# Second attention, odd steps: output tile 0 is added between the rotation's second and third operation

## What is computed

```python
q = (q_latent @ Wqb)                       # per head 64 plain + 64 rotated
r_even = x_even * cos - x_odd * sin        # the rotation of q's second half
r_odd  = x_odd * cos + x_even * sin
scores = (q @ k.T) * scale                 # causal, softmax over keys
attn   = softmax(scores) @ v
x      = x + attn @ Wo                     # summed over the heads
```

## Time and profile before

| | us |
|---|---|
| median of 3 runs | 2337.33 (2334.87 to 2339.34) |
| the profiled execution, its own time | 2336.27 |
| its span in the trace | 2334.5 |
| TensorE busy | 2239.7 (96% of the span) |
| TensorE weight loads busy | 1939.0 (83%) |
| VectorE busy | 1823.8 (78%) |
| ScalarE busy | 1202.2 (51%) |
| GpSimd busy | 938.5 (40%) |

### The profile page before, as it was taken

The page is one execution under the profiler, slowest core; times in us unless marked ns, Lnnn a source line. Parts: engine busy times, 40 slices in busy tenths (PEclk is TensorE's granted clock), DMA queues, the critical chain, the costliest instruction groups (busy, mean ns, idle before and its releaser), DMA issues. The chain is left out here.

```text
span 2334.5 us, 41914 instructions
## 1 busy us (share of the span) xinstructions
PE 2239.7 (96%) x12798; PEld 1939.0 (83%) x12798; DVE 1823.8 (78%) x4052; ACT 1202.2 (51%) x2803; POOL 938.5 (40%) x757
## 2 busy tenths in 40 slices
PE   7999999999999999999999889999999999988997
PEld 6888888888888888887897668888888888867895
DVE  7777777777777777876676769998999898986776
ACT  4555555555554555552434356566566566642434
POOL 6444444456444434355222333243334243344223
PEclk9999999999999999999999999999999999999999
DMA  3455555545433332226984100000000000017876
GB/s 129 175 202 201 201 191 180 180 165 186 143 114 118 118 118 103 95 93 247 317 279 178 54 20 1 20 20 19 0 19 19 0 19 10 27 72 262 293 252 241
DMA packets 106767, 296.63 MB, mean 127 GB/s; under 512 B 9480, under 2 KB 11912, under 8 KB 101024
## 3 DMA queue, kind: packets, MB, share of 16 engines
q1 hardware_dynamic: 85792, 239.61, 29.6%
q0 software_dynamic: 11360, 37.76, 4.1%
q10 hardware_dynamic: 9504, 17.85, 2.3%
HBM read 150.20 MB, written 144.98 MB: 126 GB/s over the span
## 5 line engine op out<-in xcount | busy, mean ns | idle before, releaser
L74 PE MATMUL bank<-wo_hi,hq_hi 128*128 128x512 f32 x576 | 234.6, 407 | 15.2 <-DVE x L1514 14.6
L74 PE MATMUL bank<-xT_hi,w_hi 128*128 128x512 f32 x584 | 232.8, 399 | 8.1 <-DVE xT_lo L202 5.0
L76 PE MATMUL bank<-xT_hi,w_lo 128*128 128x512 f32 x584 | 229.7, 393 | 0.0
L75 PE MATMUL bank<-xT_lo,w_hi 128*128 128x512 f32 x584 | 229.4, 393 | 0.0
L76 PE MATMUL bank<-wo_hi,hq_lo 128*128 128x512 f32 x576 | 226.4, 393 | 0.0
L75 PE MATMUL bank<-wo_lo,hq_hi 128*128 128x512 f32 x576 | 225.6, 392 | 0.0
L1604 POOL TENSOR_TENSOR qf<-ra,rb 64x512 f32<-64x512 f32 x64 | 82.4, 1287 | 327.0 <-DVE rb L1707 326.7
L1427 ACT ACTIVATE s<-s,top 128x128 f32<-128x128 f32 (+3 forms) x256 | 141.0, 552 | 97.5 <-DVE top L1506 97.5
L862 DVE SCALAR_TENSOR_TENSOR x<-bank,inv,x 128x512 f32<-128x512 f32 x256 | 179.8, 742 | 13.3 <-PE bank L76 13.3
L1514 DVE SCALAR_TENSOR_TENSOR x<-bank,inv,x 128x512 f32<-128x512 f32 x256 | 179.8, 743 | 3.0
L873 DVE TENSOR_TENSOR hq_lo<-bank,hq_hi 128x512 fp32r<-128x512 f32 (+1 forms) x144 | 80.3, 567 | 116.1 <-ACT arena L729 60.9
(11 more groups left out here) (348 smaller groups left out, 7282.5 us busy)
## 6 DMA issues: line engine op xcount, KB each, us to landing
sorted_x<-blank SPq DMA_DIRECT2D x48, 1584.0 KB, 11.4
arena<-split_w SPq DMA_DIRECT2D x32, 1024.0 KB
split_w<-arena SPq DMA_DIRECT2D x48, 512.0 KB, 3.2
w_raw<-dram_wa SPq DMA_DIRECT2D x32, 512.0 KB, 4.9
raw<-dram_wr SPq DMA_DIRECT2D x24, 512.0 KB, 5.7
wo_raw<-dram_woa SPq DMA_DIRECT2D x32, 256.0 KB, 4.2
ctok<-dram_wva SPq DMA_DIRECT2D x16, 512.0 KB, 5.2
arrived<-routed_y SPq DMA_DIRECT2D x8, 1024.0 KB, 8.0
```

The lines of the kernel that those rows point to most:

```text
L74: nc.tensor.matmul(out, hi, mov_hi, start=first, stop=False)
L75: nc.tensor.matmul(out, hi, mov_lo, start=False, stop=False)
L76: return nc.tensor.matmul(out, lo, mov_hi, start=False, stop=last)
```

## The change

In odd steps that have an output to add, VectorE adds tile 0 between the second and the third multiplication of the rotation. `rotate` is split in two functions for this; the other callers still run all three in a row. In even steps the order of the work stays, but the wait for `inverted` (VectorE's own reciprocals of the step) now stands ahead of the third multiplication.

```diff
         dve.wait_ge(a.proj_done, s + 1)
         ge(dve, a.rope_added, s)
-        rotate(nc, m, m.bank[3]).then_inc(a.rope_out, 1)
+        turn_even(nc, m, m.bank[3])
         if n2:
             dve.wait_ge(a.inverted, v + 1)
-            add_output(v, bv, odd, (0, 1))
+            if odd:
+                add_output(v, bv, odd, (0,))
+        turn_odd(nc, m, m.bank[3]).then_inc(a.rope_out, 1)
+        if n2:
+            add_output(v, bv, odd, (1,) if odd else (0, 1))
         if n1:
             probs_lo(u)
```

```diff
+def turn_even(nc, m, bank):
     e, o = HALF, HALF + QUARTER
     nc.vector.tensor_tensor(m.ra[e:P, :], bank[e:P, :], m.rope[e:P, 0, :], ALU.mult)
     nc.vector.tensor_tensor(m.rb[e:o, :], bank[o:P, :], m.rope[o:P, 1, :], ALU.mult)
+
+
+def turn_odd(nc, m, bank):
+    e, o = HALF, HALF + QUARTER
     return nc.vector.tensor_tensor(m.rb[o:P, :], bank[e:o, :], m.rope[e:o, 1, :], ALU.mult)
```

More of the change, by code:

```diff
@@ L1699, in ge @@
         eng.wait_ge(sem, value)
-def rotate(nc, m, bank):
+def turn_even(nc, m, bank):
     e, o = HALF, HALF + QUARTER
@@ L1706, in rotate @@
     nc.vector.tensor_tensor(m.rb[e:o, :], bank[o:P, :], m.rope[o:P, 1, :], ALU.mult)
+def turn_odd(nc, m, bank):
+    e, o = HALF, HALF + QUARTER
     return nc.vector.tensor_tensor(m.rb[o:P, :], bank[e:o, :], m.rope[e:o, 1, :], ALU.mult)
+def rotate(nc, m, bank):
+    turn_even(nc, m, bank)
+    return turn_odd(nc, m, bank)
 LATE_TILES = 2
```

## The result

The changed kernel takes 2348.95 us (median of 5 runs, 2347.47 to 2350.29), the kernel before 2335.27 us beside it (also the median of 5 runs): a ratio of 1.0054, 95% interval 1.0043 to 1.0065. It is slower by 13.7 us. The spans of the two profiled executions say the same, 2347.9 against 2334.5 us. The prediction was 2350, slower, by 13.5.

A forecast was written before the change was run, and what follows sets the result against it. TensorE's matmuls, filling 635.9 of 648 us, were taken as the bound. Losses of 3.0 + 5.5 + 0.1 + 4.9 = 13.5 us and no gain made 2350 us, slower, in a range of 2344 to 2355.

The forecast's parts named there:

- No gain: Odd steps, batches 1 to 3: tile 2 starts 0.53 us earlier, but tile 3 waits for addition 1, 0.06 more.
- VectorE's times: VectorE's odd steps: rotation ends 0.78 us later, tile 0 is added 0.7 earlier, tile 1 0.11 later.
- lost overlap: VectorE: an operation on other partitions than its forerunner waits for its end, costing about 0.1 us.
- case without the lost overlap: Rival: on VectorE, changing partitions costs nothing; 9.8 us slower in all, 2346 us; chance 0.14.
- Batches 1 and 2: 16 odd steps: the scores' load waits for GpSimd's late q_lo, 0.19 us a step, 3.0 us in all.
- Batch 3: Seven odd steps with the next pair's weights: GpSimd's queue without slack delays the scores 0.78 us each, 5.5 in all.
- Batch 0: Seven odd steps: combine waits for the later rotation, 0.70 us each, 4.9 us in all.
- The sum: All kinds of steps together: 3.0 + 5.5 + 0.1 + 4.9 = 13.5 us slower.
- step 63's 0.1: The last pair's batch 3 step: like batches 1 and 2, its successor waiting for something else anyway, 0.1 us lost.
- rivals with a free start: Tile 2's standstill goes and nothing replaces it: 0.53 us in 24 steps, 12.7 us, 2324 us; chance 0.04.
- half of the steps gaining: Rival: 14 steps lose 10.4 us, but 16 steps keep 0.53 (8.5 us); +1.9 us, 2338; chance 0.07.
- restart at every new wait: Rival: TensorE pays 0.1 us more at each of 30 new waits, 3 us more, 2353 us; chance 0.15.

The follow-up runs named there:

- late signal: Kernel before, VectorE's order kept, but in odd steps GpSimd's sum and, in batch 0, combine also wait for tile 0's addition: 2350.23 us against 2337.86.
- low partitions: Changed kernel with the third multiplication of the 31 odd steps on partitions 0 to 31, part of the rotation left out: 2345.12 us against 2337.86 for the kernel before.
- both early: Changed kernel with both additions, tiles 0 and 1, ahead of the third multiplication in the 31 odd steps: 2372.34 us against 2338.07 for the kernel before.
- runs with ScalarE: Kernel before, with ScalarE taking tile 0 from its bank and GpSimd adding it: in 16 steps 2328.68 us, in 24 steps 2325.97, in 48 steps 2321.20.

## Why the prediction was right

**No gain.** Right: tile 3's load, which stood 0.06 behind addition 1 before, was the next wait in line. The 0.53 us are found again there, as 0.54, and the load itself is 0.11 later in the step than before. The late signal shows it from the other side: with the additions in their old places and the standstill at tile 2 the steps are equally long to within 0.05.

**VectorE's times.** Forecast 0.78, 0.7 and 0.11 us (rotation late, tile 0 early, tile 1 late); measured 0.78, 0.72 and 0.12. The lost overlap was the term that made 0.78 of 0.67. The Trainium skill's rule (VectorE: DVE Perf Modes, Two Vector instructions with no wait between them) had been weighed against the rows there; the multiplication on low partitions bears it out, with 0.11 to 0.12 us a change. One reading beside it was loose: the third multiplication's forerunner does not lie on partitions from 0 on, as the prediction has it; it reads from partition 96 and writes from 64, where the third reads from 64 and writes from 96. It is a change of partitions all the same. I had priced the case without the lost overlap at 9.8 us in all; that run's 61 steps are 8.3 us longer than those of before.

**Batches 1 and 2.** Forecast 0.19 us a step, 3.0 in all; measured 0.14, 2.3 in all, which is 0.12 in fourteen steps and 0.30 in the two of the first pair (below). Two signals were too dear. ScalarE followed `qf` by 0.09 (1575.39 + 1.27 = 1576.66, then 1576.75) and not by the 0.16 of the even step, so q's rest ended 0.67 later in the step (8.40 against 7.73) and not 0.72; and TensorE heard GpSimd in 0.04 to 0.06 us where I took the bound of 0.08. Together that makes the 0.12. That the rotation's chain is enough for this loss without tile 3 was argued and is now shown by the late signal (10.75 with addition 1 in its place).

**Batch 3.** Forecast 0.78 a step, 5.5; measured 0.72, 5.0. Most of the difference is the same short signal: q's rest ends at 1535.02, the load comes at 1535.06, 0.04 behind, where it was 0.08 in the step shown before. The cause, GpSimd's queue, is shown by the run that changes its order.

**Batch 0.** Forecast 0.70 a step, 4.9; measured 0.75, 5.2. Here a reading was wrong. The prediction took 1549.35, where the combined weights' load stood before, for the end of the transposes, and put the new load 0.06 behind the rotation. But the load stands 0.11 to 0.12 behind the rotation's end in all seven steps of both kernels (1549.24 to 1549.35, then 1553.41 to 1553.52), and also where the rotation ends at 4.82 or 5.61 of the step (low partitions, both early). Free of any wait, a load behind the transposes comes at 4.21 of the step (tile 2 in the runs with ScalarE), and this one stood at 4.28 before: it followed the rotation already and moved by the whole 0.78. That the forecast was only 0.05 off is in part luck. Why it is 0.11 here and 0.05 at tile 2 stays open; a count kept in a register is not the reason, since the written-out step of the last pair, whose counts are fixed in the code, has 0.12 too.

**The sum.** 2.3 + 5.0 + 5.2 = 12.5 us in the steps, with step 63's 0.1 (forecast 0.1) 12.6, where 13.5 was forecast; the medians differ by 13.7 and the spans by 13.4. About 0.4 us of the spans' difference lies before the steps and 0.3 behind step 63's share, where nothing was changed; I count that as scatter. So the mechanism was right and its terms 0.9 us too dear in sum; the misses of the parts had both signs and partly cancelled, and that the medians come within 0.2 us of the forecast is luck. The rivals with a free start, and with half of the steps gaining, are refuted by the run that changes batches 1 and 2 alone: it should have been 8 us faster and is slower. A further 0.1 us for a restart at every new wait did not show either: in batch 3 the scores' load comes 0.74 later in the step (9.08 against 8.34) and the step is 0.72 longer.

## What to carry to other kernels

The total of the bounding engine's longest wait is not what its removal is worth: look for the wait behind it, which shows in the rows as a load or an operation that starts a few hundredths of a us after its releaser, without any idle time to its name. An engine at 91% between two consumers is not helped by a swap in its order; what one consumer gets earlier the other gets later, and a chain over three engines with 0.6 us of room does not bear 0.8. Here the remedy was to take one operation out of that engine's row and give it to two engines with gaps, and the gaps had to be found in the step's timeline.

## What was not expected of the hardware

Two steps of the first pair (batches 1 and 2) were 0.30 to 0.31 us longer than in the kernel before, the other fourteen 0.12. There the step after checks the latents first, two waits long met; the scores' load came 0.22 us after q's rest had ended (1424.79 + 1.30 = 1426.09, then 1426.31) instead of 0.05 to 0.06. The trace puts the time down to no releaser:

```profile
1424.79 1.30 POOL L1618 TENSOR_TENSOR hq_lo<-qf,hq_hi 128x512 fp32r<-128x512 f32 x1 [0.80 <-ACT hq_hi L1462]
```

```profile
1426.31 0.19 PEld L74 LDWEIGHTS bank<-xT_hi,hq_hi 128*128 128x128 f32 x1 [0.16 <-issue]
```

Behind q's rest of step 63 it is 0.22 to 0.23 us again in the changed kernel, and there too two other waits stand in front of the scores. In the kernel before, where q's rest ended 0.6 us ahead, these two steps of the first pair are no longer than the others (10.57 against 10.59). So it seems that waits that are met cost nothing while TensorE's queue is ahead, and about 0.08 us each once it has run dry. That this is their price was not tried by itself.
